# Splitting attention weights once and reloading their parts, and a rotation whose high part is a copy on ScalarE

## The chip, the cores and the metric

The kernel runs on one core of a Trainium2 chip. The metric is the device time of one execution in microseconds (us), the median of several. The engines are TensorE (PE, with PEld for its weight loads), VectorE (DVE), ScalarE (ACT), GpSimd (POOL) and SyncE (SP); SP issues all transfers. A measurement of this kernel spreads by about 0.1%: the three runs of the kernel before lie between 2510.96 and 2513.03 us.

## The reference

A transformer layer over 4 sequences of 1024 tokens and 256 channels, in float32. A layer norm feeds two branches, whose results are added to the input:

```python
xn = layernorm(x)
# attention, 16 heads of 128
qkv = einsum('bsd,od->bso', xn, w_qkv)         # w_qkv: 6144 x 256
q, k = rope(q), rope(k)                        # x * cos + rotate_half(x) * sin
attn = softmax(einsum('bqhd,bkhd->bhqk', q, k) / sqrt(128))
a = einsum('bso,do->bsd', attn @ v, w_out)     # w_out: 256 x 2048
# feed-forward, weights quantised to MXFP4 in blocks of 32
f = gelu(xn @ mxfp4(up) + up_bias) @ mxfp4(down) + down_bias
y = x + a + f
```

The weights are the same for all four sequences.

## The kernel before

Everything is written out by hand: each engine has its own instruction stream, and semaphores order the streams. Matmuls that need float32 accuracy take their operands in two parts: a high part, which is the value written as type F32R, and a low part, which is the value less the high part. Three products (high by high, high by low, low by high) are summed.

**Pairs, rounds and steps.** Attention goes by pairs of heads: 8 pairs a sequence, 32 in all. A pair has 8 steps, so two pairs make a round of 16 steps, and there are 16 rounds; a round is one turn of a loop, with the first steps (`PEELED` = 4) and the last written out. The text counts steps from 0 to 15 in a round; k8 is the step modulo 8. Each step handles a chunk of 256 queries of one head. On TensorE a step k issues, in this order: the first scores tile of the next chunk (128 queries by 1024 keys, six matmuls), what stands in slot 0, the second scores tile, the output projection of chunk k-2 (`w_ps`), what stands in slot 1, and the values of chunk k-1 (`o_ps`, 16 matmuls). A scores tile lies in one of two banks `s_ps`; it can be written once the exponential of the tile two before has been taken from its bank.

**Projections.** The 12 projections of the next pair are spread over the slots by the table `GROUPS`. Eight are for queries and keys and have to be rotated; they are numbered 0 to 7 here, as `qk_number` does, and called rotation 0 to 7. They stand in steps k8 = 3 (two), 4, 5, 7 (two), 0 and 1. Rotation 6 is in slot 0 of k8 = 0, rotation 7 in slot 0 of k8 = 1. Step k8 = 2 has no projection at all. Slot 1 of step 5 and of step 13 hold transposes for the layer norm and for the quantised weights.

**A rotation.** ACT copies a projection from its bank to `rope_a` and, with halves exchanged, to `rope_b` (`take_group`, three copies). Then `rotate` issues five operations on POOL: multiply by cos, multiply by sin, add into the high part, the same add again into `rope_a` in full, and the subtraction that gives the low part. The last one raises `qk_ready`, for which the scores of that head wait. `rope_a` and `rope_b` have two buffers, so rotation m can only be taken once m-2 is finished. The first six rotations of all are done ahead of the loop.

**Weights.** For each pair, SP loads the raw weights (`load_part` for `w_qkv` in three pieces, `load_wo` for `w_out` in two), ACT writes the high part (`w_high`, `wo_high`) and POOL the low part (`w_low`, `wo_low`). This is done for each of the 32 pairs, though pairs 8 apart have the same weights. In POOL's stream `w_low` of the piece qk0 stands at the start of k8 = 0, ahead of rotation 6.

**ACT.** In step k ACT does, in this order: weight pieces, the high part of the attention output (`high_out`, which waits for the values), the take of slot 1 of the step before, the exponential of tile 2k+2, the take of slot 0, the exponential of tile 2k+3.

**VectorE** does the maxima, the transposes of the exponentials (`turn`), low parts and sums of the output, and in some steps pieces of the layer norm and of the quantisation (`quantise`, by the table `MX_PARTS`; step 8 has parts 4 and 5). **SP** issues for each chunk eight moves `keys_first<-turned_blocks` and, between them, the loads.

## Time and profile before

| | |
|---|---|
| median of 3 runs | 2511.87 us (2510.96 to 2513.03) |
| profiled execution, own time | 2514.25 us |
| its span, first to last instruction | 2512.4 us |
| TensorE busy | 2457.9 us, 98% |
| VectorE busy | 2023.0 us, 81% |
| POOL busy | 1841.8 us, 73% |
| ACT busy | 1351.9 us, 54% |
| transfers | 354.30 MB, the queue's packets 54.3% of 16 engines' span |

The span is the profiled execution from its first to its last instruction. Times within it are counted from its start. Attention lasts to about 2380 us, the feed-forward follows. A line of the timeline gives start and duration of one instruction, or of several alike in a row (x6), and in brackets the idle time of its engine before it with what ended it. Instructions of TensorE overlap, so a group's duration includes the tail of its last one; the distance between starts is what counts. Line numbers are those of the kernel before.

### The profile page before, as it was taken

Reading aid. Unit: us, or ns where it says so; the run is one execution under the profiler, and the core shown is the slowest. Engines: PE = TensorE matmul, PEld = TensorE weight load, DVE = VectorE, ACT = ScalarE, POOL = GpSimd, SP = SyncE. Lnnn points to the kernel's source line nnn. Section 1 sums busy time; section 2 is a strip of 40 time slices with the busy share of each in tenths; the row PEclk is TensorE's granted clock in tenths of the full one; section 3 lists DMA queues with packets and bytes.
Section 4 is the critical chain, followed back from the end, with each engine's and each line's share of the span. In section 5 each row is a group of like instructions: output and inputs, shape, how many; then the busy total and the mean of one; then the engine's idle time right before and its main releaser. Section 6 shows DMA issues by size and latency. Waiting matters only on the chain. (4 is left out here: it accounts for less than half of the span.)

```text
span 2512.4 us, 41984 instructions
## 1 busy us (share of the span) xinstructions
PE 2457.9 (98%) x12656; PEld 2133.9 (85%) x12656; DVE 2023.0 (81%) x3204; ACT 1351.9 (54%) x2518; POOL 1841.8 (73%) x1485
## 2 busy tenths in 40 slices
PE   6999999999999999999999999999999999999899
PEld 5788888888888888888888888888888888888788
DVE  7778878787887878788787878878787887878677
ACT  6455555554555555555556555555555555555333
POOL 7678777777877777787777778777777877787131
PEclk9999999999999999999999999999999999999999
DMA  4455555556655555556655555556565555555742
GB/s 120 125 135 131 140 134 142 134 145 159 163 140 135 141 134 145 135 130 169 163 146 135 145 136 130 140 133 167 146 168 138 130 140 133 140 127 126 230 143 68
DMA packets 233876, 354.30 MB, mean 141 GB/s; under 512 B 37856, under 2 KB 95584, under 8 KB 233696
## 3 DMA queue, kind: packets, MB, share of 16 engines
q1 hardware_dynamic: 233824, 353.72, 54.3%
q8 instruction: 18, 0.29, 0.0%
q14 instruction: 34, 0.28, 0.0%
HBM read 66.26 MB, written 18.87 MB: 34 GB/s over the span
## 5 line engine op out<-in xcount | busy, mean ns | idle before, releaser
L921 PE MATMUL o_ps<-keys_first,v_rows 128*128 128x256 f32 x4096 | 928.5, 380 | 7.9 <-DMA keys_first<-turned_blocks 7.9
L595 ACT ACTIVATE probs<-s_ps,neg_max 128x1024 f32<-128x1024 f32 x512 | 571.4, 1116 | 676.6 <-DVE neg_max L693 671.9
L921 PEld LDWEIGHTS o_ps<-keys_first,v_rows 128*128 128x128 f32 x4096 | 764.4, 190 | 108.6 <-DMA keys_first<-turned_blocks 9.6
L921 PE MATMUL s_ps<-seq_parts 128*128 128x512 f32 x3072 | 835.9, 408 | 20.7 <-ACT probs L595 11.1
L693 DVE TENSOR_REDUCE neg_max<-s_ps 128x1 f32<-128x1024 f32 x512 | 610.8, 1203 | 165.2 <-PE s_ps L921 165.1
L921 PEld LDWEIGHTS s_ps<-seq_parts 128*128 128x128 f32 x3072 | 576.5, 189 | 145.1 <-ACT probs L595 18.4
L705 DVE STREAM_TRANSPOSE turned_blocks<-probs 128x512 f32<-128x512 f32 x1024 | 663.1, 685 | 18.5 <-DVE mx_q L779 3.7
L471 POOL TENSOR_TENSOR rope_a<-rope_a,cos 128x512 f32<-128x512 f32 x253 | 328.7, 1299 | 452.2 <-ACT rope_b L587 452.0
L921 PE MATMUL slot_ps<-seq_parts,w_parts 128*128 128x512 f32 x1506 | 388.1, 393 | 4.6 <-DMA seq_parts<-xnt_parts 4.5
L476 POOL TENSOR_TENSOR rope_a<-rope_a,rope_b 128x512 f32<-128x512 f32 x253 | 326.7, 1291 | 19.9
L474 POOL TENSOR_TENSOR seq_parts<-rope_a,rope_b 128x512 fp32r<-128x512 f32 x253 | 326.5, 1291 | 19.9
L478 POOL TENSOR_TENSOR seq_parts<-rope_a,seq_parts 128x512 fp32r<-128x512 f32 x253 | 326.3, 1290 | 19.8
L921 PEld LDWEIGHTS slot_ps<-seq_parts,w_parts 128*128 128x128 f32 x1506 | 279.4, 189 | 64.2 <-DMA seq_parts<-xnt_parts 5.8
L472 POOL TENSOR_TENSOR rope_b<-rope_b,sin 128x512 f32<-128x512 f32 x253 | 332.7, 1315 | 0.0
L601 ACT ACTIVATE o_hi<-o_ps 128x256 fp32r<-128x256 f32 x256 | 98.5, 385 | 385.7 <-PE o_ps L921 385.5
L717 DVE TENSOR_TENSOR o_lo<-o_ps,o_hi 128x256 fp32r<-128x256 f32 x256 | 105.5, 412 | 223.5 <-ACT o_hi L601 223.5
L728 DVE SCALAR_TENSOR_TENSOR y<-w_ps,inv_sum,y 128x256 f32<-128x256 f32 x512 | 224.3, 479 | 30.5 <-DVE inv_sum L712 7.7
L921 PE MATMUL slot_ps<-w_parts,seq_parts 128*128 128x256 f32 x1524 | 203.0, 283 | 0.8 <-DVE ln_lo L854 0.8
L921 PEld LDWEIGHTS slot_ps<-w_parts,seq_parts 128*128 128x128 f32 x1524 | 193.7, 191 | 3.8 <-DVE ln_lo L854 1.0
L586 ACT ACTIVATE rope_b<-slot_ps 64x512 f32<-64x512 f32 x251 | 149.5, 596 | 3.0
L587 ACT ACTIVATE rope_b<-slot_ps 64x512 f32<-64x512 f32 x251 | 148.3, 591 | 2.9
L585 ACT ACTIVATE rope_a<-slot_ps 128x512 f32<-128x512 f32 x251 | 148.0, 590 | 0.6 <-POOL seq_parts L478 0.3
(108 smaller groups left out, 2137.3 us busy)
## 6 DMA issues: line engine op xcount, KB each, us to landing
keys_first<-turned_blocks SPq DMA_DIRECT2D x2048, 128.0 KB, 2.7
w_raw<-in_w_qkv SPq DMA_DIRECT2D x96, 256.0 KB, 3.2
seq_parts<-xnt_parts SPq DMA_DIRECT2D x14, 1024.0 KB, 7.9
wo_raw<-in_w_out SPq DMA_DIRECT2D x64, 128.0 KB, 2.5
y<-in_x SPq DMA_DIRECT2D x16, 256.0 KB, 3.2
ln_x<-in_x SPq DMA_DIRECT2D x16, 256.0 KB, 3.4
xnt_parts<-ln_hi SPq DMA_DIRECT2D x16, 256.0 KB, 2.8
xnt_parts<-ln_lo SPq DMA_DIRECT2D x16, 256.0 KB, 3.1
```

The costliest lines, as they stand in the source:

```text
L471: engine.tensor_tensor(a, a, cos[:, cols], ALU.mult).then_inc(own, 1)
L472: engine.tensor_tensor(b, b, sin[:, cols], ALU.mult).then_inc(own, 1)
L474: engine.tensor_tensor(hi, a, b, ALU.add).then_inc(own, 1)
L476: engine.tensor_tensor(a, a, b, ALU.add).then_inc(own, 1)
L478: return engine.tensor_tensor(lo, a, hi.bitcast(F32), ALU.subtract)
L586: nc.scalar.activation(b[0:h], bank[h:P], ACT.Copy, scale=scale)
L587: nc.scalar.activation(b[h:P], bank[0:h], ACT.Copy, scale=scale).then_inc(rope_in, 1)
L595: nc.scalar.activation(probs[:, k2 % 4, :], s_ps[k2 % 2][:, :], ACT.Exp, bias=neg_max[:, col:col + 1], accum_out=row_sum[:, col:col + 1]). ...
L693: nc.vector.tensor_reduce(neg_max[:, k2 % 16:k2 % 16 + 1], s_ps[k2 % 2][:, :], AXX, ALU.max, negate=True).then_inc(max_ready, 1)
L705: last = nc.vector.transpose(turned_blocks[:, k % 2, 2 * half:2 * half + 2, :, n, :].rearrange("p b j q -> p j b q"), keys)
L728: last = nc.vector.scalar_tensor_tensor(rows, w_ps[:, n * DIM:(n + 1) * DIM], inv_sum[:, col:col + 1], rows, ALU.mult, ALU.add)
L921: ins = nc.tensor.matmul(out, w, m, start=(n == 0), stop=(n == len(terms) - 1))
```

## The change

**Weights.** In the first sequence (pairs 0 to 7, rounds 0 to 3) the weights are loaded and split as before, and SP also stores both parts to two tensors in DRAM (`store_part`, `store_wo`). From the second sequence on SP loads the parts from there straight into `w_parts` and `wo_parts` (`reload_part`, `reload_wo`); ACT and POOL have no weight work then. `wo_hi` and `wo_lo` become one tensor, so that one transfer takes both. The stream of each of ACT and POOL has two loops now, one that splits and one that does not (`steps_splitting`).

**Rotation.** From rotation 6 of the first pair on, POOL multiplies, multiplies and adds into `rope_a` (`rotate_rest`). ACT then writes the high part as a copy of `rope_a` (`rotated_high`), and POOL subtracts it to get the low part. The add is done once. The copy for slot 0 stands on ACT in the next step, ahead of the first exponential; the copy for slot 1 stands behind the second exponential of the next step.

The diff, cut to its core:

```diff
+            def store_part(p, part):
+                sp.wait_ge(w_ready[part], (p + 1) * 16)
+                sp.dma_start(w_split[p][:, :, :, PARTS[part]],
+                             w_parts[:, :, :, PARTS[part]].bitcast(F32)).then_inc(w_stored[part], 16)
+            def reload_part(p, part):
+                sp.wait_ge(w_stored[part], PAIRS_PER_SEQ * 16)
+                sp.wait_ge(proj_ready, (p - 1) * PAIR_GROUPS + USED[part])
+                sp.dma_start(w_parts[:, :, :, PARTS[part]].bitcast(F32),
+                             w_split[p % PAIRS_PER_SEQ][:, :, :, PARTS[part]]).then_inc(w_ready[part], 16)
...
-                        if not (last and j >= PAIRS_PER_SEQ - 2):
-                            load_part(p + 2, (j + 2) % PAIRS_PER_SEQ, "qk0")
...
+                    for at, part in ((0, "qk0"), (2, "v"), (4, "qk1")):
+                        if k8 == at and PAIRS_PER_SEQ <= p + 1 < PAIRS:
+                            reload_part(p + 1, part)
+                        if k8 == at + 2 and p + 1 < PAIRS_PER_SEQ:
+                            store_part(p + 1, part)
+                            if p + 2 < PAIRS_PER_SEQ:
+                                load_part(p + 2, p + 2, part)
...
+            def rotate_rest(p, part, n):
+                m = qk_number(part, n)
...
+                done = p * 8 + m - FIRST_ROTATED
+                pool.wait_ge(rope_in, p * 8 + m + 1)
+                nc.gpsimd.tensor_tensor(a, a, cos[:, cols], ALU.mult).then_inc(rope_mult, 1)
+                nc.gpsimd.tensor_tensor(b, b, sin[:, cols], ALU.mult).then_inc(rope_mult, 1)
+                pool.wait_ge(rope_mult, done * 2 + 2)
+                nc.gpsimd.tensor_tensor(a, a, b, ALU.add).then_inc(rope_sum, 1)
+                pool.wait_ge(rope_hi, done + 1)
+                nc.gpsimd.tensor_tensor(qk_lo[:, head, kind, cols], a, qk_hi[:, head, kind, cols].bitcast(F32),
+                                        ALU.subtract).then_inc(qk_ready, 1)
...
-                more = not (last and k >= 8)
+                more = splitting and not (isinstance(p, int) and p + 1 >= PAIRS_PER_SEQ)
...
+            def rotated_high(p, part, n):
...
+                act.wait_ge(rope_sum, p * 8 + m - FIRST_ROTATED + 1)
+                nc.scalar.activation(qk_hi[:, head, kind, half * HALF:(half + 1) * HALF], rope_a[:, m % 2, :],
+                                     ACT.Copy).then_inc(rope_hi, 1)
...
+                    g_rotated = None if first and k == 0 else group_at(k - 1, 0, last)
+                    if g_rotated and g_rotated[1] != "v":
+                        rotated_high(i * 2 + g_rotated[3], g_rotated[1], g_rotated[2])
                     if not (last and k == 15):
                         exponentials(t + 2, 2 * k + 2, first and k == 0)
...
                         exponentials(t + 3, 2 * k + 3, first and k == 0)
+                    if g_before and g_before[1] != "v":
+                        rotated_high(i * 2 + g_before[3], g_before[1], g_before[2])
```

**ACT, from the second exponential of step 8 to the second of step 9**, in the loop. Before (L595 exponential, L601 `high_out`, L571 the take of a value projection, L585 to L587 the take of rotation 7):

```order
L595 ACTIVATE probs,row_sum<-s_ps,neg_max 128x1024 [waits max_ready]
L601 ACTIVATE o_hi<-o_ps 128x256 [waits o_ready]
L569 REGISTER_ALU
L571 ACTIVATE v_rows<-slot_ps 128x512 [waits proj_ready]
L592 ISA
L593 REGISTER_ALU [waits blocks_turned]
L595 ACTIVATE probs,row_sum<-s_ps,neg_max 128x1024 [waits max_ready]
L569 REGISTER_ALU
L581 REGISTER_ALU [waits proj_ready]
L585 ACTIVATE rope_a<-slot_ps 128x512 [waits qk_ready]
L586 ACTIVATE rope_b<-slot_ps 64x512
L587 ACTIVATE rope_b<-slot_ps 64x512
```

After, in the loop of the second to fourth sequence (L689 exponential, L695 `high_out`, L680 `rotated_high`):

```order
L689 ACTIVATE probs,row_sum<-s_ps,neg_max 128x1024 [waits max_ready]
L680 ACTIVATE seq_parts<-rope_a 128x512 [waits rope_sum]
L695 ACTIVATE o_hi<-o_ps 128x256 [waits o_ready]
L655 REGISTER_ALU
L657 ACTIVATE v_rows<-slot_ps 128x512 [waits proj_ready]
L680 ACTIVATE seq_parts<-rope_a 128x512 [waits rope_sum]
L686 ISA
L687 REGISTER_ALU [waits blocks_turned]
L689 ACTIVATE probs,row_sum<-s_ps,neg_max 128x1024 [waits max_ready]
L655 REGISTER_ALU
L667 REGISTER_ALU [waits proj_ready]
L671 ACTIVATE rope_a<-slot_ps 128x512 [waits qk_ready]
```

Two copies have come in, for rotation 5 ahead of `high_out` and for rotation 6 ahead of the first exponential; each waits for POOL's add.

**POOL, from the end of rotation 5 to the start of rotation 6** (k8 = 0). Before, in the loop (L478 the subtraction, L486 `w_low` of the next pair's qk0, L471 to L478 rotation 6):

```order
L478 TENSOR_TENSOR seq_parts<-rope_a,seq_parts 128x512 [waits rope_step]
L485 REGISTER_ALU
L486 TENSOR_TENSOR w_parts<-w_raw,w_parts 128x2x256 [waits w_hi_qk0]
L470 REGISTER_ALU
L471 TENSOR_TENSOR rope_a<-rope_a,cos 128x512 [waits rope_in]
L472 TENSOR_TENSOR rope_b<-rope_b,sin 128x512
L473 ISA
L474 TENSOR_TENSOR seq_parts<-rope_a,rope_b 128x512 [waits rope_step]
L475 REGISTER_ALU
L476 TENSOR_TENSOR rope_a<-rope_a,rope_b 128x512 [waits rope_step]
L477 REGISTER_ALU
L478 TENSOR_TENSOR seq_parts<-rope_a,seq_parts 128x512 [waits rope_step]
```

After, in the loop of the first sequence (L563 the subtraction, L570 `w_low`, L558 and L559 the multiplies, L561 the add):

```order
L563 TENSOR_TENSOR seq_parts<-rope_a,seq_parts 128x512 [waits rope_hi]
L569 REGISTER_ALU
L570 TENSOR_TENSOR w_parts<-w_raw,w_parts 128x2x256 [waits w_hi_qk0]
L557 REGISTER_ALU
L558 TENSOR_TENSOR rope_a<-rope_a,cos 128x512 [waits rope_in]
L559 TENSOR_TENSOR rope_b<-rope_b,sin 128x512
L560 ISA
L561 TENSOR_TENSOR rope_a<-rope_a,rope_b 128x512 [waits rope_mult]
L562 REGISTER_ALU
L563 TENSOR_TENSOR seq_parts<-rope_a,seq_parts 128x512 [waits rope_hi]
```

One add has gone from each rotation, and each subtraction now waits for ACT's copy. In the loop of the later sequences L570 is absent too, and rotation 6 follows rotation 5 directly.

## Rows read from the trace of the kernel before

**Rows 1.** The page's first part: busy time, share, instructions of each engine.

```profile
PE 2457.9 (98%) x12656; PEld 2133.9 (85%) x12656; DVE 2023.0 (81%) x3204; ACT 1351.9 (54%) x2518; POOL 1841.8 (73%) x1485
```

**Rows 2.** Waits of TensorE, 60 to 2360 us: waiter <- releaser: us, times, longest.

```profile
PE s_ps L921 <- ACT probs L595: 10.4, 16, 0.7
PE s_ps L921 <- POOL seq_parts L478: 4.9, 1, 4.9
PE slot_ps L921 <- DMA seq_parts<-xnt_parts: 4.5, 3, 2.0
```

**Rows 3.** Timeline, steps 0 to 2 of round 6: start, us, engine, line, tiles.

```profile
925.53 0.59 ACT L587 ACTIVATE rope_b<-slot_ps 64x512 f32<-64x512 f32 x1
...
936.94 1.12 ACT L595 ACTIVATE probs<-s_ps,neg_max 128x1024 f32<-128x1024 f32 x1 [2.32 <-DVE neg_max L693]
...
939.87 1.11 ACT L595 ACTIVATE probs<-s_ps,neg_max 128x1024 f32<-128x1024 f32 x1
...
927.11 1.29 POOL L471 TENSOR_TENSOR rope_a<-rope_a,cos 128x512 f32<-128x512 f32 x1
928.36 1.29 POOL L472 TENSOR_TENSOR rope_b<-rope_b,sin 128x512 f32<-128x512 f32 x1
929.73 1.28 POOL L474 TENSOR_TENSOR seq_parts<-rope_a,rope_b 128x512 fp32r<-128x512 f32 x1
...
932.59 1.28 POOL L478 TENSOR_TENSOR seq_parts<-rope_a,seq_parts 128x512 fp32r<-128x512 f32 x1
933.83 1.30 POOL L486 TENSOR_TENSOR w_parts<-w_raw,w_parts 128x512 fp32r<-128x512 f32 x1
...
941.64 3.12 PE L921 MATMUL s_ps<-seq_parts 128*128 128x512 f32 x12
...
942.99 1.77 PE L921 MATMUL s_ps<-seq_parts 128*128 128x512 f32 x7
...
944.60 0.28 PE L921 MATMUL w_ps<-wo_hi,o_hi 128*128 128x256 f32 x1
```

**Rows 4.** Timeline, steps 8 to 10 of the same round, POOL, VectorE, ACT, TensorE.

```profile
1003.86 1.27 POOL L476 TENSOR_TENSOR rope_a<-rope_a,rope_b 128x512 f32<-128x512 f32 x1
1003.96 4.30 DVE L779 SCALAR_TENSOR_TENSOR mx_q<-mx_abs,mx_q 128x256 f32<-128x256 f32 x3
...
1005.20 1.34 POOL L478 TENSOR_TENSOR seq_parts<-rope_a,seq_parts 128x512 fp32r<-128x512 f32 x1
...
1006.51 1.48 POOL L486 TENSOR_TENSOR w_parts<-w_raw,w_parts 128x512 fp32r<-128x512 f32 x1
...
1007.95 1.47 POOL L471 TENSOR_TENSOR rope_a<-rope_a,cos 128x512 f32<-128x512 f32 x1
...
1014.17 1.74 PE L921 MATMUL s_ps<-seq_parts 128*128 128x512 f32 x6
...
1014.80 0.41 DVE L779 SCALAR_TENSOR_TENSOR mx_q<-mx_abs,mx_q 128x256 f32<-128x256 f32 x1
1015.30 1.12 ACT L595 ACTIVATE probs<-s_ps,neg_max 128x1024 f32<-128x1024 f32 x1
...
1016.56 1.66 PE L921 MATMUL s_ps<-seq_parts 128*128 128x512 f32 x6 [0.65 <-ACT probs L595]
```

**Rows 5.** Groups by line and form: busy us, mean ns of one, idle before.

```profile
L478 POOL TENSOR_TENSOR seq_parts<-rope_a,seq_parts 128x512 fp32r<-128x512 f32 x253 | 326.3, 1290 | 19.8
...
L557 ACT ACTIVATE w_parts<-w_raw 128x512 fp32r<-128x512 f32 x96 | 59.3, 619 | 0.0
```

**Rows 6.** Timeline at the start of attention: POOL's add of rotation 6, TensorE's longest wait.

```profile
56.50 1.31 POOL L474 TENSOR_TENSOR seq_parts<-rope_a,rope_b 128x512 fp32r<-128x512 f32 x1
...
67.16 2.90 PE L921 MATMUL s_ps<-seq_parts 128*128 128x512 f32 x6 [4.94 <-POOL seq_parts L478]
```

**Rows 7.** Stretch 66.5 to 73.4: busy (x) of PE, PEld, DVE, ACT, POOL, clock, DMA, GB/s.

```profile
66.50:73.40 6.90, 6.24 (x15) 4.98 (x16) 1.23 (x1) 1.94 (x4) 3.11 (x4) 0.51 0.72 171
```

**Rows 8.** Transfers by tile: issues, KB each, median us from issue to landing.

```profile
keys_first<-turned_blocks SPq DMA_DIRECT2D x2048, 128.0 KB, 2.7
```

More of the change, by code:

```diff
@@ L512, in _, with step @@
                 rotate(pool, nc.gpsimd, 0, "qk1", n, "pool", n + 2).then_inc(qk_ready, 1)
-            def step(i, k, first, last):
+            def step(i, k, first, last, splitting):
                 if k >= 16:
@@ L535, in step @@
                         p = i * 2 + g[3]
[L536 to L538 removed]
+                        rotate_rest(p, g[1], g[2])
+            steps_splitting(pool, step)
             pool.wait_ge(bias_loaded, 32)
@@ L626, in _, with step @@
             exponentials(1, 1, True)
-            def step(i, k, first, last):
+            def step(i, k, first, last, splitting):
                 c = i * 16 + k
@@ L631, in step @@
                 p = i * 2 + k // 8
-                more = not (last and k >= 8)
+                more = splitting and not (isinstance(p, int) and p + 1 >= PAIRS_PER_SEQ)
                 tail = last and k >= 16
@@ L1104, in slot @@
                     if num == 0:
-                        pe.wait_ge(w_lo_ready[part], i * 2 + ahead + 1)
+                        pe.wait_ge(w_ready[part], (i * 2 + ahead + 1) * 16)
                     if place == 0 and ahead == 2:
```

99 lines of the change are left out of this document (71 added, 28 removed).

## Prediction

> **What bounds the kernel now.** The first part of the page comes first: TensorE is busy for 98% of the span, every other engine for less [rows 1]. So the time can only fall by what TensorE idles, and it rises by whatever makes TensorE idle more. The waits of TensorE between 60 and 2360 us come next [rows 2]: 16 times for an exponential on ACT (10.4 us), once for 4.9 us for a rotated key, three times for the loads of the next sequence (4.5). With a few smaller waits this is under 25 us, 1% of the time. That is the ceiling of any gain here, whatever is taken off POOL.
>
> The timeline then tells which waits recur. A step is one of 16 in a round: two scores tiles, up to two projections, the output and the values of earlier chunks. Call T(k) the start of the first scores tile of step k. All 16 waits for ACT stand at one place, the second scores tile of step 10. In the round shown, that tile could start 1.57 us after T(10) = 1014.17, as the tile of step 2 does (its six matmuls start at 942.99 + 0.23 = 943.22, which is 1.57 after T(2) = 941.64) [rows 3]. It starts at 1016.56 [rows 4], 0.82 late. Steps 2 and 10 are the only ones without a projection between their two tiles, so the second tile comes 1.57 us after T there and some 2.9 elsewhere; a late exponential of the step before shows there first.
>
> Why is step 10 late and step 2 not? In step 8 VectorE has four operations of the quantisation (three L779 take 4.30 us, 1.43 each, while POOL works; the same form takes 0.41 when POOL is idle) [rows 4]. They push maximum, exponential, take of the projection and second exponential (at 1015.30) back.
>
> **What the change removes.** (1) Each of the 250 rotations in the loops loses one of five POOL operations, 1.29 us [rows 5]: 8 a pair, 10.3 us of some 73. (2) From the second sequence on, POOL loses the low parts of the weights (1.30 each as at 933.83 [rows 3]) and ACT their high parts (0.62 [rows 5]). Neither engine bounds the kernel, so the busy time itself is worth nothing; only the order in time counts.
>
> **What it adds: a round trip.** A rotation is now multiply, multiply, add on POOL, then a copy on ACT (0.62, taken from the weights' copy, the same 128x512 from SBUF [rows 5]), then the subtraction on POOL, which waits for the copy. ACT waits for the add, and behind that wait stand an exponential, the taking of the next projection and the second exponential. The worst place is where rotations 5, 6 and 7 of a pair follow one another, in steps 0 to 2 and 8 to 10.
>
> I put the chain together from rows of step 0 [rows 3]. Successive POOL operations are 1.24 apart from the subtraction to the next multiply (932.59 to 933.83), 1.25 between the multiplies (927.11 to 928.36), 1.37 up to the add that depends on them (928.36 to 929.73); the add takes 1.28. That is 5.14 from one subtraction to the next add's end. A dependence costs 1.37 - 1.25 = 0.12, so I take 0.1 for each hop between engines.
> - ACT has taken rotation 5 at 925.53 + 0.59 = 926.12; the copy of rotation 4 ends at 926.74, and POOL subtracts at 926.84.
> - The add of rotation 5 ends at 931.98, its copy at 932.70, POOL subtracts at 932.80.
> - The add of rotation 6 ends at 937.94, its copy at 938.66. The first exponential of step 1, now at 936.94, can start only then, 1.72 later. The second moves from 939.87 to 941.59.
> - TensorE can use the bank 1.26 after such a start (1015.30 to 1016.56 [rows 4]), at 942.85. The tile would start at 943.22, its weights some 0.2 before. So 0.2 to 0.4 us is left: **no stall in step 2**, but the cover is thin.
>
> **Step 10, second to fourth sequence.** The same chain stands there at the same distance from T, and 1014.17 - 941.64 = 72.53 is added: the copy of rotation 6 ends at 1011.19, the second exponential starts at 1014.12, against 1015.30. On VectorE two of the four operations fit into the time in which POOL waits for ACT, so that side is ready by about 1014.0 too. Where a waiting VectorE operation slips in between two POOL operations that do not depend on each other, POOL's distance is 1.44 in place of 1.24 (1006.51 to 1007.95); between dependent ones it stays 1.34 (1003.86 to 1005.20) [rows 4]. One or two of these add 0.3: the exponential starts at 1014.42, the bank is free at 1015.68, the weights wanted at 1015.54. A stall of 0.15 remains of 0.82, **a gain of 0.67** in 12 rounds: -8.0. In two of these the next step waits for the next sequence's load [rows 2], whose time does not move: 1.3 is given back.
>
> **First sequence.** Here POOL still computes the low part of the first weights (1.30) between rotations 5 and 6, in seven of eight pairs. In step 2 that gives 1.3 - 0.3 = 1.0 of stall in three rounds (the first is the start, below): +3.0. In step 10, 0.15 + 1.3 = 1.45 against 0.82 in three rounds: +1.9. The last pair of the sequence has no such part, and its gain goes into the wait for the load.
>
> **Start.** TensorE now idles 4.94 us before 67.16 [rows 6]: the six matmuls there take 2.90, where step 2 has 12 in 3.12 [rows 3]. From 66.5 to 73.4 the granted clock is 0.51, the lower level (1.2 GHz), after the 4.94 us of idle; of 6.24 us of TensorE's work in it half, 3.1 us, is the price [rows 7]. With the change ACT stands behind the add of rotation 6 (56.50 + 1.31 = 57.81) in step 1: the exponential behind it starts at 58.5, the bank is free at 59.8, and TensorE's idle time of about 5 us comes one step earlier; a second wait, for the next exponential, follows, and step 3 starts at about 68.2 in place of 67.16. If the clock falls again after that idle time, some 3 us come again, less what the second wait hides. I take 0, between -2 and +2.
>
> **Transfers.** A pair moves 2 MB of parts in place of 1 MB of raw weights, in pieces issued after a chunk's eight key moves. Those moves land in 2.7 us [rows 8] and are wanted a step later. All weights come at least two steps before use, the waits ahead of them on SP's queue have long been met, and each added issue takes some 0.6 us of a step of 7 to 10. I take 0; the bound is 1 us at each of some 24 pairs.
>
> **The sum.** -8.0 + 1.3 + 3.0 + 1.9 + 0 = -1.8. The profiled execution took 2514.25 (span 2512.4); the median of the three shown is 2511.87. The difference carries over: **2510.1 us**.
>
> **A rule weighed.** The rows say that a VectorE operation with two SBUF inputs waits for POOL, and that POOL loses at most 0.2 by it. The Trainium skill, SBUF — State Buffer, section "SBUF: two separate sides", says more: the shared port pair is an exclusive lock, and whoever comes second is blocked for the whole instruction. By this rule POOL would lose 0.41 at each such operation; it is rival C. The distances between POOL operations speak against it in this kernel.
>
> **Rivals.**
> - B, slower: the round trip is longer than I make it. A hop of 0.2 in place of 0.1, or a copy that waits, makes the chain (four hops and two copies) 0.5 longer. It decides from 0.3 on. Then 15 places in step 2 lose 0.2 and 15 in step 10 lose 0.5: +3.0 + 7.5, less 1.0 at the loads, so about 2519.6. For it: ACT has never waited for POOL in mid-chain in this trace, so no row prices that hop. Against it: the dependence on POOL itself costs 0.12.
> - C, slower: quantisation operations hold POOL for 0.41 each, three of them in the chain before step 10: +1.2 in 12 rounds, less what is given back: about 2522. Against it stand the distances above.
> - D, faster: the half rate does not come back at the start (-2), the stall of step 10 goes entirely (-0.15 x 12 = -1.8) and the next sequence's load comes earlier, since no weight load shares its step (-1.3): 2505.
> - E, slower: the parts' transfers do not hide, and keys come 1 us late once a pair: about 2534. The queue is busy for half of the time only.
> - F: the change does not take work off a path at all, since the new wait simply replaces POOL's: this is A with 0 in place of -8.0 + 1.3, 2516.8, the upper edge of no change.
>
> **Chances.** A (within 5 us of 2510.1) 0.45; B 0.20; D 0.20; C 0.06; E 0.03; F 0.06. The likeliest case alone spans 2506 to 2515. The range that leaves out two in ten is 2503 to 2520.5: it takes in B and D, not C and E. A measurement of this kernel can tell about 0.2%, 5 us, from no change. Faster than 2506.9: D and the lower edge of A, 0.26. Slower than 2516.9: B, C, E and half of F with a little of A's edge taken off B's, 0.27. Within: 0.47.
>
> **What would show it.** In the profile after, POOL's busy time falls by some 450 us and ACT's rises by some 90, with TensorE's unchanged. Right: TensorE's waits for ACT at step 10 are 0.2 or less after the first sequence and about 1.4 in it, and new waits of about 1 us stand at step 2 of the first sequence only. Wrong for B: waits for ACT at step 2 in all sequences. Wrong for C: POOL distances over 1.6 in step 8. ACT's copies wait for the add in steps 1, 5, 9 and 13; waits for moved keys in mid-sequence would speak for E. The prediction fails most easily on the 0.2 to 0.4 us left at step 2: each 0.1 beyond costs 1.5 us there and as much in step 10.

## The result, and the profile after

The changed kernel takes **2505.39 us** (median of 14 runs, 2502.06 to 2508.09), the kernel before 2512.87 (14 runs, 2510.96 to 2515.8): a ratio of 0.9970, 95% interval 0.9962 to 0.9978. That is 7.5 us faster, where 1.8 were forecast. The profiled execution took 2508.02 us with a span of 2506.2, which is 6.2 less than before's on both counts. The first part of its page, and its line on the queue that carries the transfers:

```profile
PE 2457.5 (98%) x12656; PEld 2139.8 (85%) x12656; DVE 1982.2 (79%) x3204; ACT 1437.6 (57%) x2648; POOL 1392.9 (56%) x1115
...
q1 hardware_dynamic: 267232, 395.67, 59.9%
```

Against [rows 1] POOL has lost 449 us, ACT gained 86, VectorE lost 41, and TensorE's work is the same. The 449 us off POOL bring 7.5. TensorE's waits between 60 and 2360 us, which answer to [rows 2]:

```profile
PE s_ps L1020 <- ACT probs L689: 7.5, 8, 3.3
PE o_ps L1020 <- DMA keys_first<-turned_blocks: 5.8, 1, 5.8
PE slot_ps L1020 <- DMA seq_parts<-xnt_parts: 4.8, 3, 1.9
```

The 16 waits for an exponential have become 8, two of them at the start (3.3 and 0.7, where before POOL was waited for) and six in the first sequence. One wait for moved keys, 5.8 us in the last round, is larger than any there before.

Steps 0 to 2 of round 6 in the changed kernel, in the form of [rows 3] (start, us, engine, line, tiles):

```profile
935.66 0.63 ACT L680 ACTIVATE seq_parts<-rope_a 128x512 fp32r<-128x512 f32 x1 [3.31 <-POOL rope_a L561]
...
936.20 1.10 ACT L689 ACTIVATE probs<-s_ps,neg_max 128x1024 f32<-128x1024 f32 x1
936.37 1.27 POOL L563 TENSOR_TENSOR seq_parts<-rope_a,seq_parts 128x512 fp32r<-128x512 f32 x1 [0.74 <-ACT seq_parts L680]
...
939.10 1.12 ACT L689 ACTIVATE probs<-s_ps,neg_max 128x1024 f32<-128x1024 f32 x1
...
939.38 3.12 PE L1020 MATMUL s_ps<-seq_parts 128*128 128x512 f32 x12
```

T(2) is 939.38. The copy of rotation 6 holds the exponentials back as foretold, and still both scores tiles run as one group of 12 matmuls: no stall. Steps 8 to 10, in the form of [rows 4]:

```profile
1001.10 3.46 DVE L878 SCALAR_TENSOR_TENSOR mx_q<-mx_abs,mx_q 128x256 f32<-128x256 f32 x3
...
1002.29 0.63 ACT L680 ACTIVATE seq_parts<-rope_a 128x512 fp32r<-128x512 f32 x1 [0.30 <-POOL rope_a L561]
...
1003.00 1.28 POOL L563 TENSOR_TENSOR seq_parts<-rope_a,seq_parts 128x512 fp32r<-128x512 f32 x1 [0.74 <-ACT seq_parts L680]
...
1011.82 1.12 ACT L689 ACTIVATE probs<-s_ps,neg_max 128x1024 f32<-128x1024 f32 x1
...
1011.90 3.12 PE L1020 MATMUL s_ps<-seq_parts 128*128 128x512 f32 x12
```

Here too the 12 matmuls run in one go, where [rows 4] has six, a wait of 0.65 and six. Three quantisation operations take 3.46 us, not 4.30, since one falls into the 0.74 in which POOL waits for ACT. The second exponential starts 0.08 before T(10), not 1.13 after it.

The quantisation operation ahead of the three gains too, before and after:

```profile
1002.85 1.08 DVE L803 TENSOR_SCALAR mx_q<-mx_q 128x256 f32<-128x256 f32 x1
```

```profile
1000.58 0.48 DVE L902 TENSOR_SCALAR mx_q<-mx_q 128x256 f32<-128x256 f32 x1
```

This gain of 0.60 comes from no pause: POOL's running instruction is over 0.92 us after the operation's start before, 0.33 after. Together the four operations end 1.43 earlier against T(10): 0.84 by the pause and 0.60 by where they meet POOL.

**The time by steps.** The sharpest view of all runs is the distance from T(k) to T(k+1), from the starts of the first scores tiles in the timeline. Apart from a few single steps it repeats within 0.1 us from round to round, so every difference can be given a place. The table has the medians over sequences 2 to 4, the values of round 1 (first sequence), the wait of step 11 in rounds 3, 7 and 11 (where the next sequence's load comes) as that step's length, and the last round. The other steps are alike in all kernels but for hundredths, save single ones at the start and end of attention and 0.17 at step 9 of the first sequence in a_probe.

| kernel | step 2 | step 6 | step 10 | step 11 | round 1: steps 2, 10 | step 11, rounds 3, 7, 11 | T(4), round 0 | T(13), round 15 | from there to the end |
|---|---|---|---|---|---|---|---|---|---|
| before | 6.93 | 9.81 | 7.86 | 9.68 | 6.93, 7.87 | 12.42, 11.09, 11.35 | 79.60 | 2351.1 | 161.4 |
| after | 6.93 | 9.81 | 6.93 | 9.68 | 7.69, 7.88 | 11.26, 11.46, 11.89 | 80.32 | 2340.4 | 165.8 |
| b_mx | 6.93 | 9.81 | 6.93 | 9.92 | 6.93, 6.93 | 9.92, 9.91, 9.96 | 78.32 | 2332.8 | 159.8 |
| w_only | 6.93 | 10.58 | 7.84 | 9.68 | 6.93, 7.84 | 11.57, 13.68, 13.44 | 78.67 | 2363.1 | 162.7 |
| w_fill | 6.93 | 9.81 | 7.84 | 9.68 | 6.93, 7.84 | 11.81, 13.88, 13.52 | 80.28 | 2355.9 | 162.5 |
| r_only | 7.70 | 9.81 | 7.89 | 9.68 | 7.71, 7.89 | 10.10, 9.84, 9.74 | 79.61 | 2355.6 | 159.6 |
| a_probe | 7.15 | 9.81 | 7.33 | 9.68 | 8.38, 8.40 | 11.43, 10.67, 11.14 | 79.95 | 2350.8 | 168.6 |
| a_wlow | 6.93 | 9.81 | 6.93 | 9.68 | 6.93, 6.93 | 11.51, 10.98, 13.92 | 77.22 | 2334.0 | 163.5 |

From before to after: 12 steps 10 of the later sequences and that of round 3 lose 0.94 each, -12.2 in all; step 2 of rounds 1 to 3 gains 0.76 each, +2.3; the start +0.7; one step 6 of round 0 that waited for the layer norm, -1.2; the waits for the next sequences' loads and the rest -0.3. That is -10.7 at T(13) of the last round, and the last stretch gives 4.5 back: -6.2, as the span says.

**How far one profile can be trusted.** Step 11 in rounds 3, 7 and 11, the start and the last stretch differ between profiles even where the instructions are the same. After, a_up and a_x have the same instructions up to round 12, but T(4) at 80.32, 80.64 and 78.52 and step 11 between 11.12 and 13.57. The granted clock tells most of it. Round 11 in the changed kernel and in a_x (stretch in us, busy us of PE, PEld, DVE, ACT, POOL, granted clock, DMA share, GB/s):

```profile
1744.70:1756.70 12.00, 10.06 (x49) 8.28 (x48) 8.51 (x13) 4.58 (x8) 3.85 (x3) 1.00 1.06 273
```

```profile
1744.70:1758.30 13.60, 11.61 (x49) 9.38 (x47) 8.51 (x14) 4.58 (x8) 3.86 (x3) 0.87 1.02 255
```

TensorE waits 1.9 and 2.0 us there and has the same 49 matmuls, but in a_x part of them ran at the lower level (1.2 GHz), for 1.55 us more of busy time; step 11 is 11.89 and 13.53. All steps 11 over 13 us in the 14 profiles have this, no shorter one has. The wait alone does not tell: round 3 of the kernel before waits 2.0 us and keeps the clock at 1.00. At the start too, a_x has a clock of 1.00 from 60 to 80 us where after and a_up have 0.83.

### The profile page after: what moved, and what is told of

It reads as the page before. It is cut to its first block and busy times, and to the rows that moved or that the text cites. A ratio compares the mean times of both kernels' runs of the same rounds, so it can differ in the third digit from the quotient of the medians.

```text
span 2506.2 us, 41398 instructions
## 1 busy us (share of the span) xinstructions
PE 2457.5 (98%) x12656; PEld 2139.8 (85%) x12656; DVE 1982.2 (79%) x3204; ACT 1437.6 (57%) x2648; POOL 1392.9 (56%) x1115
## 5 line engine op out<-in xcount | busy, mean ns | idle before, releaser
L1020 PEld LDWEIGHTS o_ps<-keys_first,v_rows 128*128 128x128 f32 x4096 | 767.7, 191 | 110.4 <-DMA keys_first<-turned_blocks 11.6
L689 ACT ACTIVATE probs<-s_ps,neg_max 128x1024 f32<-128x1024 f32 x512 | 568.7, 1111 | 247.9 <-DVE neg_max L792 241.7
L1020 PEld LDWEIGHTS s_ps<-seq_parts 128*128 128x128 f32 x3072 | 577.9, 189 | 133.6 <-ACT probs L689 12.1
L558 POOL TENSOR_TENSOR rope_a<-rope_a,cos 128x512 f32<-128x512 f32 x250 | 324.6, 1298 | 633.1 <-ACT rope_b L673 633.1
L563 POOL TENSOR_TENSOR seq_parts<-rope_a,seq_parts 128x512 fp32r<-128x512 f32 x250 | 320.5, 1282 | 288.4 <-ACT seq_parts L680 288.4
L680 ACT ACTIVATE seq_parts<-rope_a 128x512 fp32r<-128x512 f32 x250 | 157.6, 630 | 387.9 <-POOL rope_a L561 386.4
L561 POOL TENSOR_TENSOR rope_a<-rope_a,rope_b 128x512 f32<-128x512 f32 x250 | 322.9, 1292 | 19.6
L559 POOL TENSOR_TENSOR rope_b<-rope_b,sin 128x512 f32<-128x512 f32 x250 | 327.4, 1310 | 0.0
L695 ACT ACTIVATE o_hi<-o_ps 128x256 fp32r<-128x256 f32 x256 | 97.7, 382 | 333.1 <-PE o_ps L1020 333.1
L1020 PEld LDWEIGHTS w_ps<-wo_parts,o_hi 128*128 128x128 f32 x1024 | 176.2, 191 | 22.3 <-DVE o_lo L816 2.2
L1020 PE MATMUL w_ps<-wo_parts,o_hi 128*128 128x256 f32 x1024 | 194.3, 283 | 0.9 <-DVE o_lo L816 0.9
L672 ACT ACTIVATE rope_b<-slot_ps 64x512 f32<-64x512 f32 x251 | 149.2, 595 | 3.0
```

The source lines that it names most:

```text
L558: nc.gpsimd.tensor_tensor(a, a, cos[:, cols], ALU.mult).then_inc(rope_mult, 1)
L559: nc.gpsimd.tensor_tensor(b, b, sin[:, cols], ALU.mult).then_inc(rope_mult, 1)
L561: nc.gpsimd.tensor_tensor(a, a, b, ALU.add).then_inc(rope_sum, 1)
L563: nc.gpsimd.tensor_tensor(qk_lo[:, head, kind, cols], a, qk_hi[:, head, kind, cols].bitcast(F32), ALU.subtract).then_inc(qk_ready, 1)
L672: nc.scalar.activation(b[0:h], bank[h:P], ACT.Copy, scale=scale)
L680: nc.scalar.activation(qk_hi[:, head, kind, half * HALF:(half + 1) * HALF], rope_a[:, m % 2, :], ACT.Copy).then_inc(rope_hi, 1)
```

## The experiments

The theory from the profiles: the gain is the stall of step 10. It goes where POOL pauses for ACT (VectorE's quantisation operations then take less time) and where no low part of the weights stands ahead of rotation 6, so the change's two parts are needed together. The rivals: the work taken off POOL and ACT is what gains, by either part, or VectorE's order in step 8 has nothing to do with it.

| run | median us | ratio to before, 95% interval |
|---|---|---|
| b_mx | 2495.6 | 0.9932, 0.9919 to 0.9946 |
| w_only | 2527.6 | 1.0058, 1.0044 to 1.0072 |
| r_only | 2519.3 | 1.0020, 1.0010 to 1.0030 |
| a_probe | 2516.9 | 1.0015, 1.0006 to 1.0024 |
| w_fill | 2518.7 | 1.0019, 1.0010 to 1.0028 |
| a_wlow | 2498.3 | 0.9938, 0.9924 to 0.9951 |
| a_up | 2505.2 | 0.9966, 0.9952 to 0.9979 |
| a_best3 | 2492.1 | 0.9918, 0.9904 to 0.9931 |
| a_x | 2503.4 | 0.9952, 0.9938 to 0.9966 |
| a_bestx | 2491.1 | 0.9902, 0.9888 to 0.9917 |
| b_bestx | 2491.9 | 0.9910, 0.9896 to 0.9925 |
| b_256 | 2516.4 | 1.0008, 0.9998 to 1.0019 |

The kernel before was timed beside each set: 2512.9 (first four), 2514.0 (next four), 2514.7 (a_x to b_bestx), 2516.1 (b_256). All of after's later comparisons go by ratio where a us or two matter.

### b_mx: the kernel before, with VectorE's parts moved

```diff
-        MX_PARTS = {0: (0,), 5: (1,), 6: (2,), 7: (3,), 8: (4, 5), 9: (6,), 11: (7,)}
+        MX_PARTS = {0: (0,), 5: (1,), 6: (2,), 7: (3,), 8: (4,), 10: (5, 6), 11: (7,)}
```

> The kernel before, with two of the quantisation parts of steps 8 and 9 moved behind the place of the stall (step 8 keeps part 4, parts 5 and 6 go to step 10, step 9 has none). Theory (the gain of the change is the stall of step 10, which VectorE's quantisation operations in step 8 cause): the 16 waits of TensorE for an exponential at the second scores tile of step 10, 0.82 us each in round 6, disappear, and step 10 gets its second tile 1.57 after its first. That is 13 us, of which some 4 to 5 us are given back in the last round as in the changed kernel: 2504 to 2506 against 2512.9. POOL still does five operations a rotation and all weights. Rival (the gain is POOL's shorter rotation or the weight work itself): the wait moves to another step, the time stays within 1.5 us of 2512.9.

Measured: 2495.6, twice the gain of the change from one line of a table. TensorE's waits between 60 and 2360 us:

```profile
PE s_ps L921 <- POOL seq_parts L478: 5.3, 1, 5.3
PE o_ps L921 <- DMA keys_first<-turned_blocks: 4.6, 2, 3.8
```

The line for exponentials and that for the next sequence's load are both gone. So the stall of step 10 is made by VectorE's operations in step 8. POOL's five operations a rotation do not make it by their own length, but only by holding those operations (1.43 each against 0.41 in [rows 4]). The expectation was 9 us too high, for reasons that the table shows: the last stretch gives nothing back here (159.8), and the wait of step 11 goes too (-2.5, -1.2, -1.4 in rounds 3, 7 and 11, against 0.24 more in the other steps 11, where the moved parts stand in VectorE's way). The start is 1.3 earlier, within what profiles of the same instructions differ by. The next lines show why the wait goes. SP issues the load behind the key moves of chunk 9, which wait for VectorE's transposes of step 9. SP's queue in the kernel before, then in b_mx:

```profile
558.89 17.33 SPq L358 DMA_DIRECT2D keys_first<-turned_blocks  x16
576.32 0.57 SPq L302 DMA_DIRECT2D seq_parts<-xnt_parts  x1
```

```profile
555.76 14.44 SPq L358 DMA_DIRECT2D keys_first<-turned_blocks  x16
570.29 0.57 SPq L302 DMA_DIRECT2D seq_parts<-xnt_parts  x1
```

The load is out 6.0 us earlier, and T(9) of that round 3.1 us: 7.7 us after T(9) in place of 10.6.

### w_only and r_only: each part of the change alone

w_only has the stored and reloaded weights, but five operations on POOL for every rotation:

```diff
-                        rotate_rest(p, g[1], g[2])
+                        rotate(pool, nc.gpsimd, p, g[1], g[2], "pool", p * 8 + qk_number(g[1], g[2]) - 2).then_inc(qk_ready, 1)
...
-                        rotated_high(i * 2 + g_rotated[3], g_rotated[1], g_rotated[2])
...
-                        rotated_high(i * 2 + g_before[3], g_before[1], g_before[2])
```

> The changed kernel with its weights (parts stored and reloaded) but the rotation of before: five operations on POOL, no copy on ACT. Theory: in the second to fourth sequence rotation 6 follows rotation 5 without a gap, so POOL runs through the whole time in which VectorE has its four quantisation operations; they stay slow (1.4 us), the second exponential of step 9 starts as late as before, and the stall of 0.8 in step 10 stays in all 16 rounds: 2512 (2511 to 2514.5, with up to 1 us for the larger transfers). Rival (taking the weights' work off POOL and ACT is what gains): 12 of the 16 stalls are gone, 2505. Rival (transfers of 2 MB a pair cost something that the changed kernel hides): over 2515.

r_only has the new rotation, and splits weights for every pair:

```diff
-            with eng.Fori(SEQ_ROUNDS, ROUNDS - 1) as i:
-                rounds(i, False)
...
-                    for at, part in ((0, "qk0"), (2, "v"), (4, "qk1")):
-                        if k8 == at and PAIRS_PER_SEQ <= p + 1 < PAIRS:
-                            reload_part(p + 1, part)
...
+                        if not (last and j >= PAIRS_PER_SEQ - 2):
+                            load_part(p + 2, (j + 2) % PAIRS_PER_SEQ, "qk0")
```

> The changed kernel with its rotation (three operations, a copy on ACT, the subtraction) but weights loaded and split for every pair as before. Theory: POOL's low part of the weights now stands between the subtraction of rotation 5 and rotation 6 in all pairs, so every round looks like a round of the first sequence of the changed kernel: a stall of about 0.65 in step 2 and one of about 0.84 in step 10 (0.82 before). Against before that is 15 x 0.65 = +9.8, less what the last round hides: about 2520 (2517 to 2523), slower than before. Rival (the shorter rotation alone is what gains): 2505 to 2508.

Measured: w_only 2527.6, r_only 2519.3. **Each part alone makes the kernel slower, by 14.7 and 6.5 us, and both together make it 7.5 faster.** The waits of w_only and then of r_only:

```profile
PE s_ps L1015 <- ACT probs L689: 10.2, 16, 0.7
PE slot_ps L1015 <- DVE ln_lo L948: 6.7, 13, 0.7
```

```profile
PE s_ps L987 <- ACT probs L656: 20.9, 31, 3.4
```

r_only is as expected: 0.77 in step 2 and 0.96 in step 10, in all rounds where the low part follows. VectorE's four operations are as short there as in the changed kernel (0.48, then 3.46 for three), so it is now POOL's chain that makes the stall: ACT's copy of rotation 6 starts 2.30 before T(10) in round 6, in the changed kernel 3.52. So the new rotation takes VectorE out of the way, and the reload takes away the weights' low part that would take its place; that is why both parts are needed. In w_only the 16 stalls of step 10 stay, as expected, but a wait that no theory had named stands in step 6: for the low part of the layer norm, 0.77 a round in sequences 2 to 4, +9 us in all. The place it comes from is the end of step 5, where VectorE has five small quantisation operations (128x8). In w_only (POOL first):

```profile
974.68 1.27 POOL L537 TENSOR_TENSOR rope_a<-rope_a,cos 128x512 f32<-128x512 f32 x1
975.90 1.28 POOL L538 TENSOR_TENSOR rope_b<-rope_b,sin 128x512 f32<-128x512 f32 x1
```

```profile
974.47 0.28 DVE L881 TENSOR_SCALAR mx_amax<-mx_amax 128x8 f32<-128x8 f32 x1
974.78 1.20 DVE L883 TENSOR_SCALAR mx_amax<-mx_amax 128x8 uint32<-128x8 uint32 x1
976.01 1.20 DVE L885 TENSOR_SCALAR mx_half<-mx_amax 128x8 f32<-128x8 f32 x1
...
977.48 1.10 DVE L887 TENSOR_SCALAR mx_inv<-mx_inv 128x8 f32<-128x8 f32 x1
```

The same five in the changed kernel, where POOL pauses:

```profile
972.38 0.16 DVE L886 TENSOR_SCALAR mx_amax<-mx_amax 128x8 f32<-128x8 f32 x1
972.58 0.17 DVE L888 TENSOR_SCALAR mx_amax<-mx_amax 128x8 uint32<-128x8 uint32 x1
972.79 0.17 DVE L890 TENSOR_SCALAR mx_half<-mx_amax 128x8 f32<-128x8 f32 x1
```

An operation of 0.17 us takes 1.20, until POOL's running instruction is over: 974.78 + 1.20 = 975.98 against 974.68 + 1.27 = 975.95. The kernel before pays part of this price too: its five take 0.19, 0.17, 1.12, 0.20 and 0.96.

### w_fill: POOL work put back

```diff
+                if k8 == 4 and not splitting:
+                    nc.gpsimd.tensor_tensor(probe[:, :], cos[:, 0:2 * DIM], sin[:, 0:2 * DIM], ALU.mult)
```

> The kernel with the weights' part alone (2527.6, 14.7 over before), with one POOL operation of 128x512 added per pair in the second to fourth sequence where the low part of qk1 stood (ahead of rotation 4); its result is not used. Theory: that kernel is slower because POOL, with less work, reaches the five operations of rotation 4 some 1.3 us earlier in step 5, so that VectorE's quantisation operations there meet POOL at another point (they take 1.2 in place of 0.2), and the layer norm's low part comes 0.77 late in step 6 in 12 rounds. The filler puts POOL back: step 6 returns from 10.58 to 9.81, that is -9, to about 2518.6 (2517 to 2520). Rival (the larger transfers make it late): no change or a little slower, 2527 to 2529.

Measured: 2518.7, and step 6 back at 9.81. **Adding 1.3 us of useless work to POOL a pair of the later sequences makes the kernel 9 us faster.** It is not how much POOL does, but which of its instructions runs when VectorE's short ones come. VectorE's rows at the place, in w_fill:

```profile
974.66 0.16 DVE L884 TENSOR_SCALAR mx_amax<-mx_amax 128x8 f32<-128x8 f32 x1
974.86 0.17 DVE L886 TENSOR_SCALAR mx_amax<-mx_amax 128x8 uint32<-128x8 uint32 x1
975.07 1.12 DVE L888 TENSOR_SCALAR mx_half<-mx_amax 128x8 f32<-128x8 f32 x1
```

Two operations get through before POOL's next instruction holds the third, as in the kernel before; w_only had one. Of w_only's 14.7 us 9 are explained; in the profile most of the rest is step 11 in rounds 7 and 11 (13.7 and 13.4 in place of 11.1 and 11.4), which w_fill has too (13.9 and 13.5). In these four the granted clock is 0.87 to 0.88, before it is 1.00: TensorE is busy for 11.5 to 11.6 us there and not 9.9 to 10.0. So some 1.6 of the 2.1 to 2.8 us each is the lower clock, as in a_x. Whether the clock falls there in every run of w_only, one profile can't show.

### a_probe: how much slack the round trip leaves

```diff
+                if k8 == 0 and not first:
+                    nc.gpsimd.tensor_tensor(probe[:, :], cos[:, 0:DIM], sin[:, 0:DIM], ALU.mult)
```

> The changed kernel with one POOL operation of 128x256 more (about 0.7 us, its result is not used) between the subtraction of rotation 5 and the multiply of rotation 6 in all pairs but the first; it measures how much slack the round trip through ACT has left. Theory: 0.65 of slack in step 2 and about 0.4 in step 10 in the second to fourth sequence, so 12 x 0.1 + 12 x 0.35 = 5.4; in the first sequence, where the slack is already used up by the weights' low part, it is paid in full: 6 x 0.7 = 4.2. Sum +9.6, less 2 to 4 given back at loads and in the last round: 2511 to 2513 against 2505.4. If the slack in step 2 were only the 0.2 to 0.4 of the prediction, the sum would be 4 us more, 2515 to 2517. Rival (POOL's chain is not what these steps wait for): within 1 us of 2505.4.

Measured: 2516.9, 11.5 more. Step 2 grows by 0.22 and step 10 by 0.40 in the later sequences. The operation takes 0.74 us, but POOL's next one starts 0.70 after it (0.89 in step 9, where it meets the VectorE operation that cost the next multiply 0.2 before, so again 0.7 in all): the slack is 0.48 and 0.30. The weights' low part, which moves POOL's next start by 1.25, gives the same from the other side: 1.25 - 0.76 = 0.49 and 1.25 - 0.95 = 0.30. So POOL's chain through ACT does set these steps. The steps add up to 12 x 0.62 = 7.4 in the later sequences and 4.6 in the first, 12.1 and not the 9.6 expected, since both slacks were set too large (0.65 and 0.4). In the profile the loads and the start give 1.6 back and the last stretch adds 2.8, so nothing was given back in all (13.2 by the profile, 11.5 by the medians). The number alone would have misled: it lies within the 2515 to 2517 that the expectation kept for a slack of 0.2 to 0.4.

### a_wlow: the low part behind rotation 7

```diff
-                if k8 == 0 and more:
+                if k8 == 2 and more:
                     w_low(p + 1, "qk0")
-                if k8 == 2 and more:
                     w_low(p + 1, "v")
```

> The changed kernel with POOL's low part of the piece qk0 moved behind rotation 7 (it matters in the first sequence alone). Theory: the stalls of step 2 (rounds 1 to 3, 0.76 each) and step 10 (rounds 0 to 2, 0.95 each) of the first sequence, which the low part between rotations 5 and 6 makes, both go: -5.1, so 2500 to 2502 against 2505.4. Rival (the first sequence's stalls have another cause): unchanged within 1 us. A third outcome is a late low part at the projections of step 3, with a new wait there of up to 1 us in seven pairs.

Measured: 2498.3; all stalls of the first sequence are gone (6.93 and 6.93), and the start is 3.1 us earlier (77.22 against 80.32), which the expectation had left out. Other profiles with the low part behind rotation 7 have T(4) at 76.93 and 77.16, those of the changed kernel's start between 78.52 and 80.64, so some 1.3 us of it or more look like the edit's. No new wait came in step 3.

### a_up, a_x and b_256: the last round

a_up moves the load `up_w<-mx_blocks` (1 MB) from step 12 of the last round to step 9 of round 12. a_x moves the load of the first activations (2 MB):

```diff
-                    if last_round and k == 11:
+                    if last_round and k == 14:
                         sp.wait_ge(proj_ready, PAIRS * PAIR_GROUPS)
                         sp.wait_ge(ln_stored, ROUNDS * 32)
                         load_x(0)
```

b_256 is the kernel before with a transfer of 256 KB more ahead of that load.

> The changed kernel with the load of the first feed-forward weights (1 MB) issued in step 9 of round 12 in place of step 12 of the last round. Theory: in the last round the key moves of chunks 12 to 14 land behind two large loads, and values wait for them (5.9 and 3.0 us in the profile, more than before's 3.5 + 1.3 + 2.8 by 1.6, with the step itself 4.6 longer); with 1 MB less there 3 to 5 us come back: 2501 to 2502.5, and the runs spread less. Rival (the key moves are late by their own issue, behind the waits on the queue): unchanged within 1 us.

> The changed kernel with the load of the first feed-forward activations (two transfers of 1 MB) issued in step 14 of the last round in place of step 11. Taking 1 MB of weights out of that stretch changed nothing. Theory: it is these 2 MB, which stand directly ahead of the key moves of chunks 12 and 13, with the reload of 256 KB ahead of them that the kernel before has not, that make the values of chunks 12 and 13 late (9.8 and 20.0 after the first scores tile of step 13, against 7.4 and 15.8 before). Behind the moves of chunk 14 they delay only the last chunk's: the values come at 7.4 or less and 16, and 2 to 4 us come back: 2501.5 to 2503.5 against 2505.4. Rival: the values wait for something else, or the last chunk and the feed-forward's start lose as much: within 1 us of 2505.4, or slower if the feed-forward waits for the load.

> The kernel before with one transfer of 256 KB more (from the output weights, its data is not used) in the last round, ahead of the load of the feed-forward's first activations: the place where the changed kernel reloads a part of w_out and the kernel before loads nothing. Theory (this transfer is what makes the changed kernel's last round longer): the values of chunks 12 and 13 come at about 9.8 and 20 after the first scores tile of step 13 in place of 7.4 and 15.8, and from there to the end it is 163 to 166 us in place of 161.4; the median is 2 to 4 us over before. Rival (the key moves are late for another reason, such as where they meet the load of 2 MB, and one small transfer does nothing): within 1 us of before, values at 7.4 and 15.8.

Measured: a_up 2505.2, no change; a_x 2503.4, by ratio 0.9952 against 0.9970, whose intervals overlap; b_256 2516.4 beside 2516.1, no change that can be told, though the interval (-0.5 to +4.8 us) does not shut out the 2 to 4 that were expected. SP's queue in the last round, in the changed kernel and then in a_x:

```profile
2336.29 7.37 SPq L415 DMA_DIRECT2D keys_first<-turned_blocks  x8
2343.70 0.59 SPq L473 DMA_DIRECT2D up_w<-mx_blocks  x1
...
2344.86 18.44 SPq L415 DMA_DIRECT2D keys_first<-turned_blocks  x16
```

```profile
2344.23 12.64 SPq L415 DMA_DIRECT2D keys_first<-turned_blocks  x16
```

The 2 MB are what delays the key moves, not the 1 MB of weights: with them gone the values of chunk 12 come 3.9 us after T(13) and not 9.8, those of chunk 13 at 13.0 and not 20.0. But TensorE then waits 3.7 us for the activations at the start of the feed-forward:

```profile
PE s_ps L1121 <- DMA seq_parts<-xnt_parts: 3.7, 1, 3.7
```

So most of it only changes its name. In b_256's profile the values come at 8.7 and 17.8 (before: 7.4 and 15.8) and the end 1.8 later, somewhat under half of the way to the changed kernel; in the medians it can't be seen. With the activations loaded in step 11, the stretch from T(13) to the end is 162.5 to 168.6 us in the seven kernels that reload parts, and 159.6 to 161.4 in the three that split weights to the end. One profile each makes the reload a likely cause, not a shown one; through which transfer is open. The clock has a share in it: in the 45 us from T(13) on the granted clock is 0.96 before and 0.89 after, and from T(13) to the end TensorE is busy for 147.4 us before and 149.6 after with the same 890 matmuls. So 2.2 of the 4.5 us are longer busy time at a lower clock, the rest longer waits.

### The combinations

a_best3 is the changed kernel with a_wlow, a_up and parts 5 and 6 in steps 10 and 11; a_bestx has the activations' load in step 13 as well. b_bestx is the kernel before with the orders alone:

```diff
-        MX_PARTS = {0: (0,), 5: (1,), 6: (2,), 7: (3,), 8: (4, 5), 9: (6,), 11: (7,)}
+        MX_PARTS = {0: (0,), 5: (1,), 6: (2,), 7: (3,), 8: (4,), 10: (5,), 11: (6, 7)}
...
-                    if last_round and k == 11:
+                    if last_round and k == 13:
```

> The changed kernel with both of these and with the quantisation's part 5 in step 10 and part 6 in step 11 (step 8 keeps part 4, step 9 has none). Theory: -5.1 for the first sequence, -4 for the last round, -4 to -5 for the waits for the next sequence's load (its issue stands behind moves of chunk 9, whose transposes VectorE then does earlier), and no more to gain at step 10, which has no stall left in the later sequences: 2491 to 2494. If part 6 in step 11 makes the step 0.24 longer, as parts 5 and 6 in step 10 did in the kernel before, 3.6 are lost: 2495 to 2498.

> The combination of the changed kernel's mended parts (low part of qk0 behind rotation 7, quantisation parts 5 and 6 in steps 10 and 11, feed-forward weights in round 12) with the load of the activations in step 13 of the last round. 2492.1 was measured without the last edit. Theory: 2 to 3 us less, 2489 to 2490.5. Rival (as for the run before): 2492.

> The kernel before, with five operations a rotation and all weights split for every pair, and only orders changed: quantisation part 5 in step 10 and 6 in step 11, first feed-forward weights in round 12, activations in step 13 of the last round. Theory: 2495.6 was measured for parts 5 and 6 both in step 10; step 11 loses its 0.24 (15 x 0.24 = 3.6 less) and the last round's waits shrink by 1 to 3: 2489 to 2492. Then the change's two parts are worth nothing beyond this order, within 1.5 us of the run before. Rival (the shorter rotation gives POOL room that this order still needs): step 11 or 12 keeps a stall and it stays at 2494 to 2497.

Measured: 2492.1, 2491.1 and 2491.9. The 2 to 3 us that a_bestx was to gain on a_best3 can't be told (0.9902 against 0.9918, intervals that overlap). It and b_bestx, 0.9910, have intervals that overlap too. **With VectorE's parts placed well, splitting the weights once and the shorter rotation are worth nothing that can be measured**, though POOL is busy for 1839.0 us in b_bestx and for 1392.9 with the change. All three are faster than both kernels.

## Why the prediction was right or wrong

The time lies in the range given, at the edge of the likeliest case, and on the side called faster (under 2506.9), which had a chance of 0.26 against 0.47 for no change. The direction and the chain of causes held; four sizes did not, and one place was missing. That the number came this close is in part luck: in the profile the places for which the prediction has terms gained 10.7 us together where its sum says 1.8, and the last stretch, for which it has none, took 4.5 back.

- **What bounds the kernel.** Right: with TensorE at 98% nothing but its waits could move, and 449 us off POOL gave 7.5. The cause of the stall, VectorE's operations in step 8, is shown by b_mx.
- **The round trip.** The copy of rotation 6 right to 0.1 us, the exponential to 0.2. Laid on T(2), which comes 2.26 earlier now (939.38 against 941.64), the copy was to end at 938.66 - 2.26 = 936.40 and does at 936.29; the second exponential was to start at 939.33 and does at 939.10. A hop costs 0.08 (936.29 to POOL's start at 936.37). The slack at step 2 was sized at 0.2 to 0.4 and is 0.48, near what the start and the 1.26 and 1.57 of the prediction give alone (939.38 + 1.57 - 939.10 - 1.26 = 0.59): of the 0.2 taken off for the weights' load 0.1 was needed.
- **Step 10, later sequences, -8.0 in the sum.** The term that was mis-sized most: -11.3 measured (12 x 0.94), for two reasons. The 0.15 that was to remain is not there, but a slack of 0.3: the 0.3 added for VectorE operations between POOL's was too much (the exponential starts at 1011.82; the forecast without it is 1014.12 - 2.27 = 1011.85), and of the weights' 0.2 again only 0.1 was needed. On VectorE's side one operation fell into POOL's pause and not two, but a fourth became shorter by where it met POOL, which the prediction did not look at. And a stall of 0.82 costs 0.93 (7.86 - 6.93): behind the wait the tile's second matmul starts 0.33 after its first, and 0.23 where there is no wait. The distance between starts was the measure to take, not the lateness of one tile.
- **Given back at the loads, +1.3.** Wrong as a rule: -1.2, +0.4 and +0.5 in rounds 3, 7 and 11. The load's time was taken as fixed. It moves with VectorE's transposes, since SP issues it behind chunk 9's key moves: it is out 10.6 us after T(9) of round 3 before, 9.1 after and 7.7 in b_mx. The three sizes themselves are no larger than what profiles of the same instructions differ by there.
- **First sequence, +3.0 and +1.9.** The mechanism is right, the low part ahead of rotation 6 (a_wlow). Step 2 grew by 2.3 and not 3.0 (the slack was larger), step 10 by nothing (0.95 of stall took the place of 0.93), and round 3 took the full gain of 0.94 in step 10.
- **Start, 0.** +0.7 by T(4), and -1.2 a few steps on. TensorE's idle time came one step earlier as foretold, and the half rate with it: from 59 to 66 us the granted clock is 0.64. It did not in a_x, with the same instructions there (1.00 from 60 to 80 us, T(4) at 78.52), so the +0.7 is one outcome of at least two.

```profile
60.10 2.23 PE L1020 MATMUL s_ps<-seq_parts 128*128 128x512 f32 x6 [3.29 <-ACT probs L689]
63.02 2.92 PE L1020 MATMUL s_ps<-seq_parts 128*128 128x512 f32 x6 [0.69 <-ACT probs L689]
```

- **Transfers, 0.** Right in mid-sequence: no step but the named ones changed. Missing was the last round, +4.5, where the prediction looked at nothing. Without it the profile's -6.2 would have been -10.7.
- **Rival C**, POOL held by VectorE: wrong. In w_only POOL's starts are 1.22 apart (974.68, 975.90) beside a VectorE operation that was held for 1.20. The Trainium skill, SBUF — State Buffer, section "SBUF: two separate sides", calls the shared ports an exclusive lock, whoever is first having them for the whole instruction. The trace agrees on VectorE's side (0.17 becomes 1.20). POOL can only lose where it comes second, and its instructions follow each other so closely that it hardly does. The rule was weighed as a price for POOL; what counts is the price for VectorE.
- **Rival D**, 2505, has the size that was measured, but only one of its three reasons is right, that the stall of step 10 goes entirely (1.8 more than in the forecast by its sum, 3.3 measured). The half rate came back, and the load did not come early for lack of a weight load: in r_only, which still loads weights there, it lands 17.3 to 17.5 us after T(9), in the changed kernel 18.2 to 18.9.

## What to carry to other kernels

When one engine does 98% of the span, find the one or two steps where it waits and ask which operations of which engine are late there; moving those (one line of a table) gave more than taking 449 us off an engine that nobody waited for. Measure from start to start of the bounding engine, step by step: where the rounds repeat to 0.1 us, every edit's gain and loss can be read off, those in the places not looked at too. Where a step does not repeat, look at its granted clock, and at a second profile of the same instructions, before giving it a cause. Two parts of one change need not add: test each alone, since a part that only removes work can shift the rest into a worse meeting.

## What was not expected of the hardware

- VectorE's TENSOR_SCALAR operations on 128x8 elements take 0.17 us alone and up to 1.20 when a POOL instruction on 128x512 runs; they end with it. The RECIPROCAL of the same size among them is not held: 0.20 in all kernels. Whether the next one is short depends on where it starts: in w_fill the second begins at 974.86, in the gap of 0.07 between two dependent POOL instructions, and takes 0.17.
- So removing POOL work can slow VectorE: w_only has 125 us less of POOL work than the kernel before (1716.7 against 1841.8) and 25 us more of VectorE's (2047.9 against 2023.0) for the same 3204 instructions.
- Key moves of 128 KB land in 2.7 us (median of the program), and in 7.8 us from 2334 to 2362 us, where 4 MB of loads are in flight. Eight are issued in 5.1 us where nothing holds them. The 18.4 us of the 16 in the last round hold two waits of SP, 6.3 us for the values of an earlier chunk and 2.1 for VectorE's transposes: an issue that waits passes the delay on to all behind it.
- The same step 11, with a wait of TensorE of about 2 us, takes 11.9 us in one profile and 13.5 in another, as the granted clock stays at 1.00 or is 0.87.
